# One transpose between every two score matmuls of a streaming attention, the rest between the weighted matmuls

## The reference

```
def _L0_xattn_ref(ix, iother, W, b):
    ex = jnp.einsum('bld,ed->ble', ix, W) + b
    eother = jnp.einsum('bld,ed->ble', iother, W) + b
    scores = jnp.einsum('bld,bmd->blm', ex, eother)
    attn = jax.nn.softmax(scores, axis=-1)
    aligned = jnp.einsum('blm,bmd->bld', attn, iother)
    return aligned
...
x = x + _L0_xattn_ref(_layernorm(x, axis=-1), ctx_1024, L0_xattn_W, L0_xattn_b)
x = x + _L0_attn_ref(_layernorm(x, axis=-1), L0_attn_proj_w, L0_attn_proj_b, L0_attn_filter_time)
x = x + _L0_ffn_ref(...)
```

## Time and profile before

| what | us |
|---|---|
| median of three runs | 204.65 |
| the three runs | 204.46, 204.65, 207.01 |
| the profiled execution | 203.6 |
| its span, first to last instruction | 201.4 |
| length of one full attention step in it | 4.14 |

### The profile page before, as it was taken

How to read it: one execution, slowest core, us unless ns; L and a number is a source line. 1 busy time by engine, 2 the same in 40 slices (tenths; PEclk the granted TensorE clock), 3 DMA queues, 4 the chain that set the end, 5 groups by cost and what they waited for, 6 DMA issues and landing times.

```text
span 201.4 us, 3822 instructions
## 1 busy us (share of the span) xinstructions
PE 191.1 (95%) x1206; PEld 142.4 (71%) x1206; DVE 126.8 (63%) x270; ACT 102.7 (51%) x208; POOL 82.2 (41%) x60
## 2 busy tenths in 40 slices
PE   7499999999999999999999969989999999999994
PEld 5398999999999989999999957754335443343452
DVE  2248997788878779778877659855845422362431
ACT  2148877777677777768675330346427621122120
POOL 1209999976778768887785040000000000000000
PEclk9969999999999999999999999999999999999999
DMA  6993996885884884983691799999994999855000
GB/s 139 312 345 107 338 311 214 237 267 159 269 232 130 273 281 134 337 248 118 177 241 24 253 345 381 360 380 369 370 380 155 284 344 324 203 134 130 0 3 26
DMA packets 24906, 47.00 MB, mean 233 GB/s; under 512 B 1600, under 2 KB 11968, under 8 KB 24896
## 3 DMA queue, kind: packets, MB, share of 16 engines
q1 hardware_dynamic: 24464, 46.80, 74.0%
q10 hardware_dynamic: 432, 0.07, 0.2%
HBM read 46.73 MB, written 0.13 MB: 233 GB/s over the span
## 4 chain that ended last, share of the span: by engine, by line
PE 76%; DMA 10%; issue 6%; DVE 4%; SPq 1%; POOL 1%; ACT 1%; POOLq 0%; DVEq 0%
PE bank L385 11%; PE bank L590 10%; DMA bias<-biases_dram 6%; PE bank L426 6%; PE bank L430 6%; PE bank L398 6%; PE bank L428 6%; PE bank L402 6%; PE bank L400 6%; PE bank L604 5%; PE bank L411 5%; DMA raw<-in_ctx_dram 4%; PE bank L558 2%; PE bank L614 2%; PE bank L621 1%
## 5 line engine op out<-in xcount | busy, mean ns | idle before, releaser
L846 POOL TENSOR_TENSOR c_lo<-raw,c_hi 128x1024 fp32r<-128x1024 f32 (+1 forms) x25 | 54.0, 2159 | 21.3 <-ACT c_hi L701 20.8
L930 DVE TENSOR_TENSOR cT_lo<-bank,cT_hi 128x512 fp32r<-128x512 f32 (+1 forms) x50 | 31.8, 676 | 10.3 <-ACT cT_hi L693 8.5
L693 ACT ACTIVATE cT_hi<-bank 128x512 fp32r<-128x512 f32 (+1 forms) x48 | 25.6, 586 | 9.4 <-PE bank L385 9.4
L426 PE MATMUL bank<-c_hi,pT_hi 128*128 128x258 f32 x98 | 29.8, 304 | 0.0
L385 PE MATMUL bank<-tab,raw 128*128 128x128 f32 x196 | 26.2, 276 | 2.8 <-DMA raw<-in_ctx_dram 2.8
L430 PE MATMUL bank<-c_hi,pT_lo 128*128 128x258 f32 x98 | 27.6, 282 | 0.0
L428 PE MATMUL bank<-c_lo,pT_hi 128*128 128x256 f32 x98 | 27.5, 281 | 0.0
L841 POOL TENSOR_TENSOR c_hi<-raw,zero 128x512 fp32r<-128x512 f32 (+1 forms) x25 | 25.7, 1027 | 4.3 <-DMA raw<-in_ctx_dram 4.3
L385 PEld LDWEIGHTS bank<-tab,raw 128*128 128x128 f32 x196 | 22.6, 143 | 3.3 <-DMA raw<-in_ctx_dram 3.2
L708 ACT ACTIVATE pT_hi<-bank 128x512 fp32r<-128x512 f32 (+1 forms) x25 | 14.8, 591 | 15.4 <-PE bank L411 15.3
L398 PE MATMUL bank<-cT_hi,q_hi 128*128 128x512 f32 (+1 forms) x50 | 21.4, 429 | 0.1
(11 more groups left out here) (139 smaller groups left out, 297.1 us busy)
## 6 DMA issues: line engine op xcount, KB each, us to landing
raw<-in_ctx_dram SPq DMA_DIRECT2D x24, 512.0 KB, 4.0
bias<-biases_dram SPq DMA_DIRECT2D x16, 320.0 KB, 6.9
late_gu<-in_L_ffn_Wg_dram SPq DMA_DIRECT2D x3, 1024.0 KB, 10.7
late_gu<-in_L_ffn_Wu_dram SPq DMA_DIRECT2D x3, 1024.0 KB, 11.8
late_d<-in_L_ffn_Wd_dram SPq DMA_DIRECT2D x3, 1024.0 KB, 13.8
early_gu<-in_L_ffn_Wg_dram SPq DMA_DIRECT2D x4, 512.0 KB, 4.7
early_gu<-in_L_ffn_Wu_dram SPq DMA_DIRECT2D x4, 512.0 KB, 5.0
early_d<-in_L_ffn_Wd_dram SPq DMA_DIRECT2D x4, 512.0 KB, 5.1
```

The costliest lines, as they stand in the source:

```text
L426: nc.tensor.matmul(bank[6 + r][:, 0:D + 2], ph, c_hi[:, slot, t, :], start=(t == 0), stop=False)
L693: nc.scalar.activation(cT_hi[:, g % 2, h, 0:n], bank[h][:, 0:n], ACT.Copy).then_inc(cThi_rdy, 1)
L846: nc.gpsimd.tensor_tensor(c_lo[:, slot, 0:nt, :], raw[:, slot, 0:nt, :], c_hi[:, slot, 0:nt, 0:D].bitcast(fp32), ALU.subtract).then_inc(cl ...
L930: nc.vector.tensor_tensor(cT_lo[:, g % 2, h, 0:n], bank[h][:, 0:n], cT_hi[:, g % 2, h, 0:n].bitcast(fp32), ALU.subtract).then_inc(cTlo_rdy, 1)
```

## The change

The two transposes of each block step are taken apart and laid between matmuls, one at a time. A step now begins with the six score matmuls, each followed by one context transpose of the next group; then come the twelve weighted matmuls, with the last two context transposes behind the first two of them and the four probability transposes behind the third to sixth. The middle and last of the three score products change places, so that `cT_lo` is needed last. The scores wait for `cT_hi` and `cT_lo` chunk by chunk and no longer for both chunks. On ACT `rows_hi` moves behind `exps`. On DVE `running_max` moves between the two chunks of `ctx_lo`. No instruction is added or dropped.

```
            def transpose_ctx(loop, g, j):

                h, t = j // GT, j % GT
                nt = GT if loop is not None else tiles_of(g)
                if j == 0:
                    pe.wait_ge(ld_raw[g % RING], raw_count(loop, g))
                if t == 0 and (loop is not None or g >= 1):
                    pe.wait_ge(cTlo_rdy, twice(loop, 2 * (g - 1) + h + 1))
                if t < nt:
                    last = nc.tensor.transpose(bank[h][:, t * P:(t + 1) * P],
                                               raw[:, g % RING, t, h * P:(h + 1) * P], ident)
...
            def score(loop, g, j):

                n = (GT if loop is not None else tiles_of(g)) * P
                h, r = j // 3, g % 2
                if j == 0 and g >= 2:
                    pe.wait_ge(negm_rdy, times(loop, g - 1))
                if j == 0 and g == 0:
                    pe.wait_ge(q_rdy, 1)
                if j == 0 and loop is None and g == 1:
                    pe.wait_ge(s0_rdy, 1)
                if j % 3 == 0:
                    pe.wait_ge(cThi_rdy, twice(loop, 2 * g + h + 1))
                    nc.tensor.matmul(bank[2 + r][:, 0:n], q_hi[:, h, :], cT_hi[:, r, h, 0:n],
...
                elif j % 3 == 1:
                    nc.tensor.matmul(bank[2 + r][:, 0:n], q_lo[:, h, :], cT_hi[:, r, h, 0:n],
...
                else:
                    pe.wait_ge(cTlo_rdy, twice(loop, 2 * g + h + 1))
                    last = nc.tensor.matmul(bank[2 + r][:, 0:n], q_hi[:, h, :], cT_lo[:, r, h, 0:n],
...
            def step(loop, i):
                for j in range(6):
                    if i < GROUPS:
                        score(loop, i, j)
                    if i + 1 < GROUPS:
                        transpose_ctx(loop, i + 1, j)
                for j in range(12):
                    if i >= 2:
                        weigh(loop, i - 2, j)
                    if j < 2 and i + 1 < GROUPS:
                        transpose_ctx(loop, i + 1, 6 + j)
                    if 2 <= j < 6 and 1 <= i <= GROUPS:
                        transpose_prob(loop, i - 1, j - 2)
```

`transpose_prob` and `weigh` are cut into single instructions in the same way; their waits stay where the first of their instructions stands. The other two engines:

```diff
@@ ACT
                 if i + 1 < GROUPS:
                     ctx_hi(loop, i + 1, (GT if full else tiles_of(i + 1)) * P)
-                    rows_hi(loop, i + 1, (i + 1) % RING, GT if full else tiles_of(i + 1))
                 if 1 <= i <= GROUPS:
                     prob_hi(loop, i - 1, (GT if full else tiles_of(i - 1)) * P)
                 if i < GROUPS:
                     exps(loop, i, (GT if full else tiles_of(i)) * P)
+                if i + 1 < GROUPS:
+                    rows_hi(loop, i + 1, (i + 1) % RING, GT if full else tiles_of(i + 1))
@@ DVE
                 if i + 1 < GROUPS:
-                    ctx_lo(loop, i + 1, (GT if full else tiles_of(i + 1)) * P)
+                    ctx_lo(loop, i + 1, (GT if full else tiles_of(i + 1)) * P, (0,))
                 if i < GROUPS:
                     running_max(loop, i, (GT if full else tiles_of(i)) * P)
+                if i + 1 < GROUPS:
+                    ctx_lo(loop, i + 1, (GT if full else tiles_of(i + 1)) * P, (1,))
```

More of the change, by code:

```diff
@@ L376, in spectrum @@
                                  ).then_inc(spec_ps, 1)
[L378 to L387, removed]
@@ L403, in scores, with transpose_prob @@
                                             start=False, stop=(h == DK - 1))
[L404 to L410, removed]
+                    if h == DK - 1:
+                        last.then_inc(score_ps, 1)
+            def transpose_prob(loop, g, t):
+                nt = GT if loop is not None else tiles_of(g)
+                if t == 0:
+                    pe.wait_ge(prob_rdy, times(loop, g + 1))
+                    if g >= 2:
+                        pe.wait_ge(pTlo_rdy, times(loop, g - 1))
+                if t < nt:
@@ L411, in transpose_prob @@
                     last = nc.tensor.transpose(bank[4 + g % 2][:, t * P:(t + 1) * P],
                                                prob[:, g % 2, t * P:(t + 1) * P], ident)
[L413 to L425, removed]
+                    if t == nt - 1:
+                        last.then_inc(pT_ps, 1)
@@ new lines, in weigh @@
+            def weigh(loop, g, j):
+                nt = GT if loop is not None else tiles_of(g)
+                t, r, slot = j // 3, g % 2, g % RING
+                if t >= nt:
+                    return
+                if j == 0:
+                    pe.wait_ge(pTlo_rdy, times(loop, g + 1))
+                    pe.wait_ge(clo_rdy, times(loop, g + 1))
+                    if g == 0:
+                        pe.wait_ge(one_set, 1)
+                    if loop is not None or g >= 2:
+                        pe.wait_ge(O_upd, times(loop, g - 1))
+                ph, pl = pT_hi[:, r, t * P:(t + 1) * P], pT_lo[:, r, t * P:(t + 1) * P]
+                if j % 3 == 0:
@@ L434, in step @@
             def step(loop, i):
[L435 to L439, removed]
-                    transpose_prob(loop, i - 1, GT if loop is not None else tiles_of(i - 1))
-                if i >= 2:
-                    weigh(loop, i - 2, (i - 2) % RING, GT if loop is not None else tiles_of(i - 2))
@@ L445, in _ @@
+            for j in range(GT):
+                transpose_ctx(None, 0, j)
             pe.wait_ge(WT_rdy, DK)
@@ L451, in _ @@
                 last.then_inc(exT_ps, 1)
-            transpose_ctx(None, 0, 0, (1,))
+            for j in range(GT, 2 * GT):
+                transpose_ctx(None, 0, j)
             pe.wait_ge(exT_rdy, DK)
@@ L925, in slot_norm, with ctx_lo @@
                 last.then_inc(se_rdy, 1)
-            def ctx_lo(loop, g, n):
-                for h in range(DK):
+            def ctx_lo(loop, g, n, chunks=range(DK)):
+                for h in chunks:
                     dve.wait_ge(cThi_rdy, twice(loop, 2 * g + h + 1))
```

24 lines of the change are left out of this document (13 added, 11 removed).

## The result

| what | before | after |
|---|---|---|
| median, us (runs) | 205.43 (4, 204.46 to 207.01) | 209.25 (4, 208.66 to 210.03) |
| profiled execution, its span | 203.6, 201.4 | 209.61, 207.4 |
| predicted | | 208.8, range 205.5 to 213.5 |

The ratio is 1.018, with an interval from 1.010 to 1.027: the changed kernel is slower, and whether by more or by less than 2% the interval leaves open. Some executions of any of these kernels are disturbed and take some per cent longer; medians here are over all runs and ratios over the undisturbed ones alone, so a ratio can differ from the quotient of the two medians beside it. One more comparison of the same two kernels stands among the experiments.

What follows compares the result with a forecast made beforehand. PE's own rate was taken as the bound. The profiled 203.6 us plus 2.87 at the start, zero in the loop and 1.42 at the end gave 207.9; the lowest run gave the forecast 208.8, range 205.5 to 213.5 us.

Steps and rivals of the forecast that it cites:

- Both waits: At the start, step 1's first transpose waits for `cT_lo`, +0.55 us, and the probability transposes for the exp, +1.56 us.
- the lost cover: At the start, group 1's eight transposes no longer run during the wait for q but behind it: +0.76 us.
- the loop at zero: In the loop, the same 30 instructions take 4.15 us in any order and no new wait appears: no change.
- The price of a transpose between scores: On PE, a transpose between two score matmuls still costs 0.110 us, because the next score's weight load is not hidden.
- Rival A: In PE's steps, more than one weight set loads ahead, transposes cost 0.06 us: 195 to 196 us; chance 0.10.
- rival B: In PE's steps, each transpose-matmul edge costs about 0.01 us, 4.4 us more: 213 us; chance 0.20.
- steps of 4.14 us: In the loop, a sign that the forecast is right: each step still takes 4.14 us.
- my own threshold: In PE's steps, an edge price from 0.003 us would decide, adding over 1 us.
- The zero for ACT, DVE and SP: In the loop, the moves on ACT and DVE and SP's later reload make PE wait nowhere: zero cost.
- The start, +2.87: In steps 0 to 2, terms of 0.76, 0.55 and 1.56 us sum to 2.87; step 3 begins at 26.28.
- The end, +1.42: In steps 23 to 26, weighted matmuls wait for split probabilities, +0.25, +0.96 and +0.25 us: 10.11 against 8.69 us.
- Behind it nothing: Behind the attention, the experts' loads and the bias load of 12.06 us shift along with it: nothing added or taken off.

Runs made afterwards that it cites:

- k2: Changed kernel with PE's old block order in the loop, steps 3 to 22, only: loop 82.76 us, ratio 1.021.
- k8: Changed kernel with ACT's exps of group 0 moved between the two chunks of `ctx_hi` of group 2: start 10.52 us.
- k10: Changed kernel with step 0 of PE alone in the old block order: start 10.02 us.
- k11: Changed kernel with PE's step 0 in old block order and ACT's exps of group 0 between the chunks of `ctx_hi` of group 2: start 8.98 us.
- k4: Changed kernel with only steps 23 to 26 of PE in the old block order: end 8.98 us, span 205.3 us.
- k9: The unedited changed kernel once more, beside new runs of the kernel before: 209.26 against 203.97 us, ratio 1.025.
- k5: Changed kernel with PE's old block order and DVE's old order outside the loop: median 206.92 against 203.97 us, ratio 1.013.
- k12: Kernel before with eight unused matmuls on zeros added on PE ahead of the first context transposes: median 205.35 against 205.3 us.
- k7: Changed kernel with the loop's transposes interleaved only between weighted matmuls, the rest in blocks: step 4.153 us.

## Why the prediction was right

The forecast was 208.8 and the median 209.25. Both waits and the lost cover were foreseen and came near their sizes; one term, the loop at zero, was wrong. The steps behind it, in the prediction's order:

- **The price of a transpose between scores.** Predicted 0.110, the load of the next weights; measured 0.109 between scores and 0.232 - 0.119 = 0.113 between weighted matmuls. Rival A (195 us) fell: neither between scores nor between weighted matmuls did a transpose go for less. The loads above fit the reading of the earlier trace rows, one set ahead and no more: the transpose's weights load from 115.18, while the matmul ahead of it streams, and those of the next matmul only from 115.27, about when the transpose itself begins. In the step of the earlier trace rows the loads for the third to the sixth score and for the first transpose begin at 61.77, 62.01, 62.24, 62.47 and 62.70, each within 0.01 us of the start of the score ahead of it (61.77, 62.00, 62.23, 62.47, 62.70). Between the scores of a step PE waits for no semaphore, so the next score stood ready each time. That 0.11 is the load and not the transpose's own streaming was argued from the earlier trace rows; this row of the kernel before bears it out. It has the loads of the last matmul instructions of q, each of which moves a single column. One load is 0.19 long and the four together 0.53, so they too start 0.11 apart:

```profile
13.31 0.53 PEld L460 LDWEIGHTS bank<-col,exT 128*128 128x128 f32 x4
```

- **The loop at zero.** Wrong by 0.83 us, in the direction of rival B. I took PE's work as 6 x 0.233 + 12 x 0.119 + 12 x 0.110 "in any order". Twenty more edges a step cost 0.041 us, 0.002 each on the mean. Of the prediction's own signs, steps of 4.14 us was the one that didn't show. B named the kind of loss, at five times the size, and what makes it is not shown; my own threshold for it was 0.003. Rows of 8 and of 2 transposes bound an edge only to 0.01, and 400 edges turn that into 4 us. The zero for ACT, DVE and SP in the loop held: k2 shows 82.76, and in the changed kernel PE is busy for all 83.60.
- **The start, +2.87.** Measured +2.93. Counted from the streaming of the first score, at 14.90 where I had 15.02, everything should stand 0.12 earlier than written: step 1's first transpose at 17.96 (its start is shown at 18.00, so it streams at about 18.1), the probability transposes at 21.6 (21.64), step 3 at 26.16 (26.18). The 0.05 for the semaphore stands in no row of before; in the changed kernel a load begins 0.05 behind the end of the exp (21.47 to 21.52), 0.06 behind that of `q_lo` (14.72 to 14.78) and 0.12 behind that of `cT_lo` (17.85 to 17.97). k8 and k10 show both waits and the lost cover to be on the path. The size owes something to luck: k10 and k11 missed in the same kind of sum by 0.3 and 0.5. Counting the idle times of the timeline would have given 0.9 + 0.3 + 1.3; the 0.9 for q stood before as well, under the transposes, and isn't a loss of its own.
- **The end, +1.42.** Measured +1.47. From step 23 at 109.78 I had the weighted matmuls streaming at 114.45, 117.28 and 119.18; they do at 114.45, 117.30 and 119.20. k4 takes back 1.46 with PE's order alone.
- **Behind it nothing.** The part behind the attention took 87.18 against 86.25 in the two profiled executions. It lies between 85.7 and 88.9 in the other variants, with no clear relation to the edit (86.36 for the same kernel in k9), so I don't count this 0.9 to the change. The bias load makes it up: 13.11 against 12.06.
- **The sum.** 2.93 + 0.83 + 1.47 = 5.23, less 0.16 for an earlier first score, plus 0.93 behind the attention, is the 6.0 by which the span grew. Of the 4.29 foreseen, 4.40 came, and 0.83 of the loop on top. The medians grew by 3.8 here and by 5.3 in k9. That the forecast of the median was so near owes something to chance: the phases alone would have given 204.65 + 5.2 = 209.9, and 208.8 itself was built on the lowest run of before, not on the median.

## What to carry to other kernels

Where PE was busy without a gap, an instruction cost the greater of its streaming and the next one's load (0.110 us for a transpose of 128 columns, 0.119 for 258 columns, 0.233 for 512), to 0.003 us, whatever stood beside it, so interleaving kinds bought nothing; it cost 0.041 us a step, and took away the block that covered another engine's chain where the pipeline fills and drains. So cost a new order first at its first and last steps, and undo an order on all engines together: half of a pair of matching orders brought waits of 1.08 and 0.51 us that neither whole order has. And cut traces by phases when runs differ by more than the effect does: here phases repeat to 0.05 us where medians differ by 1 to 3. They say nothing of what stands ahead of and behind them, though, where k5 and k12 lost their time.

## What the runs showed that I had not expected

- The loop pays 0.041 us a step for twenty more edges between transposes and fp32r matmuls, beside scores and beside weighted matmuls alike. The halves pay 0.016 and 0.014, so they don't sum to it.
- The clock of the first microseconds goes with PE's idle gap before the first rows land: after 1.75 and 2.08 us of idle (k7, k11) it stayed at 1.00, and in the other traces, after 2.12 (k4) to 3.54 us (k5), it stood at 0.50 until 11 to 15.5 us of the span. With 2.08 and 2.12 on two sides, the gap alone may not be what parts them; k12, where the gap is filled, kept 1.00. The first score then lies between 4.5 and 7.0 us behind the first context transpose, a spread of half of what the change costs.
- A start that was 1.41 us sooner didn't end sooner: k12 lost 4.61 us behind the attention, 2.88 of it in a bias load of 14.94 us (12.06 before, 13.11 in the changed kernel) and 1.74 behind that load, where PE's clock was 0.94 against 0.99.
